# Adaptive layer-norm attention block on one core: gates as rows, a new prologue, other product orders

## The reference

```python
sa, ca, ga, sb, cb, gb = (mod[:, i] for i in range(6))
ga = (2 * (ga >= 0) - 1) * maximum(abs(ga), 0.25)      # gb likewise
h = layernorm(x) * (1 + ca) + sa
x = x + ga * attention(h)      # 32 query heads, 8 key/value heads of 128, rotary, causal softmax, wo
h = layernorm(x) * (1 + cb) + sb
x = x + gb * ffn(h)            # silu(x1 + b1) * (x2 + b2), then w3 and b3
```

## Time and profile before

| | us |
|---|---|
| runs (3) | 818.54, 820.6, 821.0; median 820.6 |
| profiled execution, its own time | 823.52 |
| its span, first to last instruction | 821.7 |
| TensorE busy | 782.8 (95%) |
| POOL busy | 567.1 (69%) |
| VectorE busy | 595.5 (72%) |
| ScalarE busy | 507.6 (62%) |
| mean granted TensorE clock | 0.979 |

### The profile page before, as it was taken

One profiled execution on the slowest core, in us unless ns is written; L12 is line 12 of the kernel. 1 busy time (PEld: TensorE's weight loads), 2 busy tenths in 40 slices (PEclk: granted clock), 3 DMA queues, 4 the chain that ended last, 5 costly groups with the idle time before them and its releaser, 6 DMA issues.

```text
span 821.7 us, 11551 instructions
## 1 busy us (share of the span) xinstructions
PE 782.8 (95%) x3600; PEld 634.3 (77%) x3600; DVE 595.5 (72%) x1238; ACT 507.6 (62%) x1201; POOL 567.1 (69%) x384
## 2 busy tenths in 40 slices
PE   7879989988999999999999999999999999979997
PEld 2555768877888888888888888888888877757885
DVE  6566567867777868776877777787778688558785
ACT  2624666557667866776667656776767665864341
POOL 1634595767867786778677867797858898447453
PEclk9889999999999999999999999999999999998999
DMA  9611936677667756775587657867667856988011
GB/s 314 214 50 40 273 87 181 130 187 217 151 185 200 233 139 180 193 240 149 181 195 241 145 189 191 256 160 227 150 221 179 267 149 177 268 252 228 19 52 51
DMA packets 191885, 147.14 MB, mean 179 GB/s; under 512 B 62672, under 2 KB 168272, under 8 KB 189776
## 3 DMA queue, kind: packets, MB, share of 16 engines
q1 hardware_dynamic: 191408, 146.33, 63.5%
q10 hardware_dynamic: 416, 0.07, 0.0%
HBM read 91.82 MB, written 54.53 MB: 178 GB/s over the span
## 4 chain that ended last, share of the span: by engine, by line
PE 64%; POOL 12%; ACT 7%; DVE 7%; DMA 5%; SPq 2%; issue 2%; DVEq 0%; POOLq 0%; ACTq 0%
PE q_bank L510 15%; PE out_bank L568 14%; PE s_bank L510 9%; PE o_bank L554 8%; PE x_bank L510 7%; POOL pT_lo L1372 4%; ACT probs L1142 2%; POOL rope_tmp L1398 2%; PE s_bank L756 2%; DMA spread_dram<-turned 2%; POOL wo_lo_sb L1372 2%; ACT probs L1150 2%; DMA acc<-in_L_attn_x_dram 1%; POOL qT L1372 1%; PE s_bank L769 1%
## 5 line engine op out<-in xcount | busy, mean ns | idle before, releaser
L1372 POOL TENSOR_TENSOR pT_lo<-pT_raw,pT_hi 128x1024 fp32r<-128x1024 f32 (+1 forms) x96 | 194.3, 2038 | 65.3 <-ACT pT_hi L1119 65.3
L1142 ACT ACTIVATE probs<-probs,neg_max 128x32 f32<-128x32 f32 (+15 forms) x256 | 130.6, 512 | 151.2 <-DVE neg_max L819 151.1
L1372 POOL TENSOR_TENSOR qT<-rope_tmp,qT 128x512 fp32r<-128x512 f32 x64 | 83.1, 1299 | 93.1 <-ACT qT L1119 93.1
L510 PE MATMUL s_bank<-kT,qT 128*128 128x32 f32 (+15 forms) x768 | 124.5, 311 | 6.3 <-POOL qT L1372 4.2
L510 PEld LDWEIGHTS s_bank<-kT,qT 128*128 128x128 f32 x768 | 114.8, 192 | 16.5 <-issue 4.9
L838 DVE STREAM_TRANSPOSE turned<-probs 128x512 f32<-128x512 f32 (+1 forms) x64 | 96.7, 1511 | 41.7 <-DMA spread_dram<-turned 35.5
L1398 POOL TENSOR_TENSOR rope_tmp<-rope_tmp 128x512 f32<-128x512 f32 x80 | 110.3, 1386 | 23.3 <-DVE rope_tmp L796 23.3
L1150 ACT ACTIVATE probs<-probs,row_inv 128x32 f32<-128x32 f32 (+15 forms) x256 | 111.9, 508 | 1.2 <-DVE row_inv L828 1.2
L819 DVE CUSTOM_DVE_ANT_0 probs<-s_bank,mask_sb 128x32 f32<-128x32 f32 (+15 forms) x256 | 98.5, 433 | 17.7 <-PE s_bank L510 17.3
L568 PE MATMUL out_bank<-wo_hi_sb,attn_hi 128*128 128x512 f32 x248 | 98.9, 399 | 12.3 <-POOL wo_lo_sb L1372 8.0
L510 PE MATMUL q_bank<-hT_hi,wq_hi_sb 128*128 128x512 f32 x244 | 97.4, 399 | 2.4 <-DVE rope_tmp L796 2.3
(11 more groups left out here) (252 smaller groups left out, 1612.9 us busy)
## 6 DMA issues: line engine op xcount, KB each, us to landing
spread_dram<-turned SPq DMA_DIRECT2D x64, 256.0 KB, 3.8
pT_raw<-spread_dram SPq DMA_DIRECT2D x16, 1024.0 KB, 5.9
spread_dram<-turned SPq DMA_DIRECT2D x64, 192.0 KB, 4.2
pT_raw<-spread_dram SPq DMA_DIRECT2D x16, 768.0 KB, 4.9
wq_raw<-in_L_attn_wq_dram SPq DMA_DIRECT2D x36, 256.0 KB, 4.3
wo_raw<-in_L_attn_wo_dram SPq DMA_DIRECT2D x9, 1024.0 KB, 6.0
spread_dram<-turned SPq DMA_DIRECT2D x64, 128.0 KB, 4.1
pT_raw<-spread_dram SPq DMA_DIRECT2D x16, 512.0 KB, 6.3
```

Source lines behind the costliest of these rows:

```text
L510: last = pe.matmul(dst, lhs(a, cc), rhs(b, cc), start=(k == 0), stop=(k == len(todo) - 1))
L1142: nc.scalar.activation(rows, rows, ACT.Exp, bias=neg_max[:, par, t:t + 1], scale=-1.0, accum_out=row_sum[:, par, t:t + 1]).then_inc(exp_do ...
L1372: nc.gpsimd.tensor_tensor(dst, src, hi.bitcast(f32), ALU.subtract).then_inc(done, 1)
```

## The change

- **Scores of tile 0.** The two halves of the keys lie side by side (`k_both`), one product of the query's high half streams both (2 x n columns, into two places of the bank), a second one streams the low half of the query against the high keys. VectorE first adds the mask to the second place and then takes the maxima with that sum as the mask.
- **Order of products.** In `attend` each chunk has its high products first, waiting for `pT_hi`, and then the low one behind `pT_lo`. In `project_out` at s % 4 == 0 all eight high products of wo come first.
- **Gates as rows.** Rows 5 and 2 are no longer copied and turned; VectorE computes the gate on the two rows (`gate_rows`), in slots 2 and 3 of group 0, and SP stores each with one DMA in slots 3 and 4.
- **First wo.** Loaded in slot 1 of group 0, split in slot 3.
- **Prologue.** x of the second batch is loaded before the last half of wmod 1; one unread product goes; the first keys are made in another order (`first_k`), two of the four high halves come from ScalarE; the second `turn_x` stands one query product earlier, the modulation rows 3 after the values, their turning in slot 0; VectorE has the low halves of h of batch 1 between the rotations. The first query product in group 0 no longer waits for the sixth rotation.

```diff
-                kT[s][b] = sb(f"kT_{s}{b}", [P, T], f32r)
+                kT[s][b] = k_both[b][:, s, :]
...
             load_wmod_halves(0)
-            load_wmod_halves(1)
+            load_wmod(1, slice(0, KC // 2), wmod_half_in[1])
             sp.dma_start(acc[:, TT:2 * TT, :], x_tiles[:, TT:2 * TT, :]).then_inc(x_in[2], 16)
+            load_wmod(1, slice(KC // 2, KC))
...
+                    if s == 1 and first:
+                        sp.wait_ge(mod_rows, 4)
+                        load_wo(0)
...
-                    if g == 1 and s == 0:
-                        for a in range(2):
-                            sp.wait_ge(gates_made, a + 1)
-                            for b in range(B):
-                                sp.dma_start(gates_dram[a, b, :].rearrange("(k p) -> p k", p=P), gate[:, a * KC:(a + 1) * KC, b],
-                                             allow_slow_non_contiguous=True).then_inc(gates_out, 16)
+                    if first and s in (3, 4):
+                        a = 4 - s
+                        sp.wait_ge(gates_made, s - 2)
+                        sp.dma_start(gates_dram[a, :, :], mod_row[(2, 5)[a]]).then_inc(gates_out, 16)
...
+            def first_k():
+                for k in range(KC + 1):
+                    if k < KC:
+                        pe.wait_ge(*((h_hi[0], k + 1) if k < 2 else (h_hi_act, k - 1)))
+                        for a in range(2):
+                            pe.matmul(x_bank[:, :], wk_s[a][:, k, :], hT[0][:, k, 0:T], start=(k == 0 and a == 0), stop=False)
+                    if k >= 1:
+                        pe.wait_ge(h_lo[0], k)
+                        last = pe.matmul(x_bank[:, :], wk_s[0][:, k - 1, :], hT[1][:, k - 1, 0:T], start=False, stop=(k == KC))
+                last.then_inc(k_proj, 1)
...
-                need(pe, roped, ROPE_GROUP, g, ROPE_FIRST + rope_q_at(s) - (1 if s % TT == 1 else 0))
+                if isinstance(g, int) and g == 0 and s == 0:
+                    pe.wait_ge(mod_ready, 2)
+                    turn_rows(3)
+                else:
+                    need(pe, roped, ROPE_GROUP, g, ROPE_FIRST + rope_q_at(s) - (1 if s % TT == 1 else 0))
...
+                    if i == 0:
+                        pe.matmul(s_banks[t][:, 0:2 * P].rearrange("p (a n) -> p a n", a=2)[:, :, 0:n], qT[0][b][:, t, :, :],
+                                  k_both[b][:, :, 0:n], start=True, stop=False)
+                        pe.matmul(s_banks[t][:, 0:n], qT[1][b][:, t, :, :], kT[0][b][:, 0:n],
+                                  start=False, stop=True).then_inc(scores_ready, 1)
...
+                for n, (lo, hi) in enumerate(CHUNKS[i]):
+                    done = chunks_to(s + SLOTS) - 2 * CHUNKS_UNIT + n + 1
+                    for bb, ready in enumerate((pT_hi, pT_lo)):
+                        need(pe, ready, 2 * CHUNKS_UNIT, g, done)
+                        for st_ in range(lo, hi):
+                            for a in range(2 - bb):
+                                last = pe.matmul(o_bank[:, :], v_s[a][:, b, st_, :], pT[bb][par][:, :, PLACES[par] - 1 - i + st_, :],
+                                                 start=(st_ == 0 and a == 0 and bb == 0), stop=(st_ == i and bb == 1))
...
+                todo = [(h, a, bb) for h in range(REP) for a, bb in PARTS]
+                if s % TT == 0:
+                    todo.sort(key=lambda p: p[2])
...
-            warm(1)
+            pe.wait_ge(wk_hi, 1)
             turn_rows(1)
...
+                if tile_of(s) == 0:
+                    for t in range(QT):
+                        need(dve, scores_ready, QT * SLOTS, g, QT * s + t + 1)
+                        n = width(s, t)
+                        nc.vector.tensor_tensor(
+                            prob_rows(s, t), s_banks[t][:, P:P + n].rearrange("p (j s) -> p j s", s=W32),
+                            mask_sb[:, T - n:T].rearrange("p (j s) -> p j s", s=W32), ALU.add).then_inc(scores_masked, 1)
...
+            def gate_rows(m):
+                dve.wait_ge(mod_rows, MODS.index(m) + 1)
+                if m == 2:
+                    dve.wait_ge(mod_made, 4)
+                row, x = mod_row[m], mod_banks[m][0:B, :]
+                link(nc.vector.tensor_scalar(row, x, 0.0, 0.5, ALU.is_ge, ALU.subtract))
+                link(nc.vector.scalar_tensor_tensor(out=x, in0=row, scalar=4.0, in1=x, op0=ALU.mult, op1=ALU.mult))
+                nc.vector.scalar_tensor_tensor(out=row, in0=x, scalar=0.5, in1=row, op0=ALU.max,
+                                               op1=ALU.mult).then_inc(gates_made, 1)
```

More of the change, by code:

```diff
@@ L600, in group @@
                     if makes_v(g, s):
+                        if first and s == 2:
+                            pe.wait_ge(gates_made, 1)
                         need(pe, wv_lo, 1, 0, 1 + LOAD[v])
@@ L873, in group @@
                     maxima(g, s)
+                    if first and s == 2:
+                        gate_rows(5)
                     if first and s == 3:
                         read_modulation()
+                        gate_rows(2)
                     if last and s in (1, 2):
@@ L894, in group @@
                     v = (SLOTS * g + s) // TT
[L895 removed]
+                    if first and s == 3 or r == 0 and not first and (v == 1 or fresh(v - 1)):
                         for n in range(2, REP):
[L897 removed]
+                            wo_low(LOAD[max(v, 1) - 1], n)
                     if not (first and s == 0):
@@ L1312, in _ @@
                 modulate_x(0, k)
-            wq_high(0, 1)
+            for k in range(2, KC):
+                act.wait_ge(h_ready[0], k + 1)
+                split_hi(hT[0][:, k, 0:T], h_tmp[0][k], h_hi_act)
+            for h in range(1, REP):
+                wq_high(0, h)
             act.wait_ge(norm_ready, 2)
@@ L1430, in group @@
                     v = (SLOTS * g + s) // TT
-                    if r == 0 and (s > 0 or not first) and (v == 1 or fresh(v - 1)):
+                    if first and s == 3 or r == 0 and not first and (v == 1 or fresh(v - 1)):
                         for n in range(2):
-                            wo_low(LOAD[v - 1], n)
+                            wo_low(LOAD[max(v, 1) - 1], n)
                     if not (first and s < 2):
```

160 lines of the change are left out of this document (72 added, 88 removed).

## The result

The changed kernel took 797.01 us in the median of four runs (796.46 to 797.38), against 820.8 for the kernel before (four runs): a ratio of 0.9715, 95% interval 0.9696 to 0.9734.

What follows compares the result with a forecast made beforehand. TensorE was taken as the pace, busy 388.13 of 390 us in the middle. Terms of 4.7 + 6.0 + 4.4 + 3.4 + 3.4 + 5.3 + 2.2 = 29.4 us gave a median of about 791 us, range 783 to 803.

Steps and rivals of the forecast that it cites:

- the small terms behind the first scores: Up to slot 4's attention: eight small transposes go, four come in, two score groups save 0.45 us each; 0.9 net.
- half of two low halves of h: Before the first scores: VectorE's low halves of h, 1.28 us each, two in the way, perhaps half hidden; costs 1.7 us.
- First keys to first scores: Prologue: earlier keys and modulation rows moved back bring the first scores from 51.2 to 46.5 us, a gain of 4.7.
- First scores to slot 4's attention: From 51.17 to 107.45 us: a query wait, half-clock stretches and small work go; gain 6.0 us (4.4 to 7.9).
- First wo: Output product at 107.45 to 114.61 us: earlier load and high products first remove waits and half clock; 4.4 us.
- Gates: Group 1: without stores in 4-byte pieces, SP's queue no longer delays spread, VectorE and TensorE; 3.4 us.
- Later wo and tile 0: Later groups: waits for wo covered by high products, 3.4 us, and fewer tile-0 score products, 5.3 us.
- the freed waits come back on POOL and ScalarE: Rival, 22%: other engines swallow freed waits, so only 17.5 us are gained, 803 us.
- The end: From 648 us: high attention products first and clock recovery, less four additions, gain 2.2 us (-0.7 to 5).
- Scores: Tile-0 slots: eight products replace twelve, about 0.107 us each whatever their width; 0.45 us per slot, 5.3 in all.
- The rival by width: Tile-0 scores: width sets the pace, so 5.3 us less is gained, 796 us; chance 3%.
- the slower rival: Tile-0 slots: each added VectorE addition is held behind POOL, four at 1.3 us, giving 832 us; chance 3%.

## Why the prediction was right, and where it wasn't

The forecast of 791 us lay 6 below the measured 797.0, inside its range of 783 to 803; the sum was 29.4 us against 26.7 in the traces. Terms that were too high and too low cancelled in part, so the total is closer than its parts. Some of the sums were also off by themselves: the small terms behind the first scores (0.8 - 0.4 + 0.9) make 1.3 and not 0.9, half of two low halves of h is 1.3 and not 1.7, and 12 x 0.45 is 5.4.

- **First keys to first scores, 4.7 predicted, 2.9 measured; the term that was mis-sized.** The step "the last two products at 0.43 us each put the keys at about 25.1" took the last low half of h as the bound, at 23.6 to 24.4 us. That half ended at 25.5: x landed 1.1 us earlier and not 1.7, a second small scalar operation was held (see below), and the last subtraction took 1.8 us where the three ahead of it took 0.7. And it wasn't the bound: TensorE had begun at 21.58 and needed 12 x 0.43 = 5.2 us at half clock, so it was the bound itself, until 26.82. The run with three unread products shows the other bound: its last key product begins at 25.22, just behind the last low half. The rest of the term, from the keys to the scores, came out as worked out: 21.5 us against 21.4.
- **First scores to slot 4's attention, 6.0 predicted, 7.1 measured.** I took half of the half-clock loss behind the first scores as saved; all of it went (granted clock 1.00 from 51 to 80 us). That was luck in part: of nine kernels with the new prologue, each with 2.4 us of idle time there (2.7 with its ramp), four kept the full clock and five fell. Against it, the gate on rows delayed the query product in slot 4 by 0.4 us, as forecast, and the scores of slot 4 waited 0.70 us for the low half of qT (0.19 before), which wasn't.
- **First wo, 4.4 and 4.4.** Right in size; of the two causes given only one works. The low halves of wo end at 91.3 us, the product begins at 97.5, and undoing the orders cost nothing here.
- **Gates, 3.4 and 3.7.** Right in mechanism (SP's queue, then the spread, VectorE, TensorE's addition). Put back into the changed kernel the stores cost 5.1.
- **Later wo and tile 0, 8.7 predicted, 6.0 measured; the step that failed.** The rival "the freed waits come back on POOL and ScalarE" is what the steady groups show, on POOL. I had found POOL's queue and let it take 0.38 of 0.72 per group. Slot by slot a steady group saves 1.3 us in slot 4 (the orders 0.9, the tile-0 scores 0.45) and gives 1.2 back in slot 6, at the wait of 1.05 and its slow first product. So about 0.15 of the orders' saving is kept, not 0.34, and nothing of the scores' saving in that slot; only the scores of slot 0 count in full. Groups 2 to 5 of the changed kernel are 0.5 to 0.8 us shorter than before where 0.34 + 0.9 was predicted. The saving of the scores in slot 4 had been counted in full, as if POOL's queue took nothing of it.
- **The end, 2.2 and 2.8.** The attention behind 738.58 took 4.97 us before; it now takes 3.2, from 713.47 to 716.68, with the wait for low halves inside it all but gone (0.61 to 0.08), as worked out; the idle time ahead of it stands as it was (2.51, before 2.31). The other part is the clock, which was at 0.5 from 740.0 to 746.9 before and stays at 1.00 now; why it stays was not tried. The total fits in part by luck: slot 0 of group 7 brought 1.3 us where nothing had been counted, and the next four slots gave 1.1 back.
- **Scores.** 0.44 us per slot whatever the width, as read from the 107 ns. The rival by width falls, and so does the slower rival: the four additions took 0.66 us, not 4 x 1.3, though the first stood beside a POOL subtraction (91.31 to 93.72 us), and taking them away changed nothing. The Trainium skill, TensorE: Matmul & The Clock Gate, section Back-to-back issue gap, gives 81 ns for a sustained pair of 128 columns, by which the slot would be 8 x 0.081 = 0.65 us, an estimate; the trace has 0.84.

## What to carry to other kernels

Cost a freed wait by the next wait behind it that some other queue ends: everything saved between the two is one sum, and it is taken once, up to that queue's length. Then look in that queue for an operation that nobody needs soon, and put it behind the one that is waited for: one such move was worth 4.8 us here, and doubled what the product orders are worth (4.0 to 8.0 us in the traces). And check an edit's own premise by a count that the page gives (packets, records), before its time is read.

## What I had not expected of the hardware

- **Idle time alone doesn't say whether the clock falls.** Nine kernels have the new prologue and 2.38 to 2.43 us of idle time ahead of the first scores; behind it four kept a clock of 1.00 and five fell. Six of the nine have the same program up to there, and of those four kept it and two fell. All three with unread products ahead of the keys had a clock of 1.00 there and fell at the first scores, at 47.6 to 52.8 us. Three of three against two of six makes it likely that this work moves the fall, and does not show it. The nine divide by the first stretch: where half clock began at 19.0 to 19.8 and lasted 6.8 us, none fell at the first scores (four kernels); where it lasted 3.4 us or was absent, all fell (five). Nine traces show that, they don't explain it. The Trainium skill, TensorE: Matmul & The Clock Gate, section Part 1: The HAM clock gate (the "warmup" mystery), calls the transition to the full clock variable from run to run; for the fall, the four against two in the same program are all that the traces here have.
- **Some small VectorE operations are held until POOL's end.** Two scalar operations on four columns in the changed kernel's prologue took 1.2 us each; a later one of the same line as the second, with POOL idle, took 0.16. Each of the two ended 0.02 to 0.03 us after the POOL subtraction that was on hand (those ended at 18.09 and 19.31 us). It was one such operation in the kernel before, from 17.83 to 19.05 us behind a subtraction that ended at 19.02 (the earlier trace rows has another, of 1.74 us, at the end). So 1.0 of the 1.1 us gained by the earlier x was lost. Not every small operation is held: the four that join the statistics ran in 0.15 to 0.18 us inside a POOL subtraction at 671.6 us. No run here took POOL's work away, so the cause is read from the times alone:

```profile
16.92 1.19 DVE L1020 TENSOR_SCALAR rstd<-var_eps 128x4 int32<-128x4 int32 x1
18.15 1.18 DVE L1022 TENSOR_TENSOR newton<-rstd 128x4 f32<-128x4 f32 x1
...
19.76 0.16 DVE L1022 TENSOR_TENSOR newton<-rstd 128x4 f32<-128x4 f32 x1
```

```profile
16.83 1.26 POOL L1422 TENSOR_TENSOR wk_lo_sb<-wk_raw,wk_hi_sb 128x512 fp32r<-128x512 f32 x1 [16.39 <-ACT wk_hi_sb L1169]
18.06 1.25 POOL L1422 TENSOR_TENSOR wq_lo_sb<-wq_raw,wq_hi_sb 128x512 fp32r<-128x512 f32 x1
```

- **2,048 pieces of 4 bytes cost TensorE 5 us**, through SP's queue, the spread through DRAM and VectorE, although their own issue took 2.26 us.
